# Queries of a gated cross-attention block: where they are split into high and low parts, and how they reach the stacked tile

## The reference

```python
qs = relu(layernorm(x)).reshape(bs, ts, 16, 32);  ks = vs = relu(ctx).reshape(...)
att = softmax(einsum('bthf,byhf->bhty', qs, ks) / sqrt(32))
out = einsum('bhty,byhf->bhtf', att, vs).reshape(bs, ts, -1)
x = x + tanh(g_xattn) * relu(out @ ffn_w.T + ffn_b)
h = layernorm(x);  hp = h shifted by one token
r = sigmoid((mu_r*h + (1-mu_r)*hp) @ W_r.T)
k = square(relu((mu_k*h + (1-mu_k)*hp) @ W_k.T))
x = x + tanh(g_ffn) * r * (k @ W_v.T)
```

## Time and profile before

| | |
|---|---|
| median of three runs | 2981.03 us (2979.23 to 2982.32) |
| the profiled execution | 2980.25 us, its span 2978.4 us |
| PE, matmuls | 2860.3 us busy, 96% of the span |
| PE, weight loads | 2190.6 us, 74% |
| DVE | 2330.1 us, 78% |
| ACT | 1564.3 us, 53% |
| POOL | 1045.4 us, 35% |
| DMA | 408.56 MB, mean 137 GB/s; SP's queue 39.6% of 16 engines, ACT's 7.3% |
| mean granted clock of PE | 0.993 |

### The profile page before, as it was taken

One profiled execution on the slowest core, in us unless ns is written; L12 is line 12 of the kernel. 1 busy time (PEld: TensorE's weight loads), 2 busy tenths in 40 slices (PEclk: granted clock), 3 DMA queues, 4 the chain that ended last, 5 costly groups with the idle time before them and its releaser, 6 DMA issues.

```text
span 2978.4 us, 71298 instructions
## 1 busy us (share of the span) xinstructions
PE 2860.3 (96%) x23168; PEld 2190.6 (74%) x23168; DVE 2330.1 (78%) x4175; ACT 1564.3 (53%) x2828; POOL 1045.4 (35%) x902
## 2 busy tenths in 40 slices
PE   3899999999999999999999999999999999999998
PEld 2677777777777777777777777777777777777776
DVE  5777877878878878878877877877878778788774
ACT  4445555555455455555555555555555555554552
POOL 0233333333343343333333333333333333333434
PEclk9899999999999999999999999999999999999999
DMA  5544445445445445445445445455455454454431
GB/s 168 150 122 140 144 124 155 140 127 155 135 131 156 137 131 154 133 137 150 131 142 149 128 143 153 120 149 152 120 152 146 124 152 142 124 156 137 130 109 41
DMA packets 405258, 408.56 MB, mean 137 GB/s; under 512 B 164577, under 2 KB 329441, under 8 KB 405218
## 3 DMA queue, kind: packets, MB, share of 16 engines
q1 hardware_dynamic: 352994, 340.92, 39.6%
q10 hardware_dynamic: 52224, 67.12, 7.3%
HBM read 272.64 MB, written 134.22 MB: 137 GB/s over the span
## 4 chain that ended last, share of the span: by engine, by line
PE 59%; DVE 16%; DMA 10%; SPq 7%; issue 5%; ACT 1%; ACTq 1%; DVEq 0%; POOL 0%; POOLq 0%
PE bank L951 29%; DMA out_dram<-x 8%; PE bank L918 7%; PE bank L932 6%; PE bank L906 5%; PE bank L944 4%; DVE m_nat L699 4%; DVE o_val L718 4%; SPq L272 3%; DVE st L652 3%; DVE k_raw L682 2%; PE bank L893 2%; PE bank L875 2%; SPq L258 2%; SPq L270 2%
## 5 line engine op out<-in xcount | busy, mean ns | idle before, releaser
L496 ACT ACTIVATE probs<-bank 128x512 f32<-128x512 f32 x1024 | 596.4, 594 | 455.7 <-PE bank L918 228.1
L699 DVE TENSOR_REDUCE m_nat<-bank 128x2 fp32r<-128x512 f32 x1024 | 695.4, 685 | 107.4 <-PE bank L906 106.7
L477 ACT ACTIVATE q_st<-bank 96x512 fp32r<-96x512 f32 x512 | 304.1, 594 | 718.9 <-PE bank L875 718.8
L918 PE MATMUL bank<-q_st,k_st 97*128 97x256 f32 x2048 | 449.9, 301 | 64.2 <-ACT probs L496 47.4
L718 DVE RECIPROCAL o_val<-bank 128x256 f32<-128x256 f32 x256 | 449.1, 1754 | 56.1 <-PE bank L944 51.7
L918 PEld LDWEIGHTS bank<-q_st,k_st 97*128 97x128 f32 x2048 | 341.8, 191 | 153.8 <-issue 58.5
L906 PE MATMUL bank<-k_st,q_st 96*128 96x256 f32 x2048 | 431.6, 293 | 7.4 <-DMA k_st<-k_dram 4.8
L397 POOL TENSOR_TENSOR xm<-xm 128x512 f32<-128x512 f32 x128 | 133.3, 1041 | 787.2 <-ACT xm L540 787.2
L906 PEld LDWEIGHTS bank<-k_st,q_st 96*128 96x128 f32 x2048 | 358.2, 192 | 59.8 <-issue 6.2
L708 DVE CAST m_t<-bank 4x256 fp32r<-4x256 f32 x256 | 105.1, 411 | 285.5 <-PE bank L884 285.4
L364 POOL TENSOR_TENSOR o_lo<-o_mv,o_hi 128x512 fp32r<-128x512 f32 x128 | 164.8, 1287 | 430.0 <-ACT o_hi L503 430.0
(11 more groups left out here) (90 smaller groups left out, 6026.6 us busy)
## 6 DMA issues: line engine op xcount, KB each, us to landing
k_st<-k_dram SPq DMA_DIRECT2D x256, 256.0 KB, 3.6
k_raw<-ctx_t_dram SPq DMA_DIRECT2D x256, 128.0 KB, 3.0
x_ln<-x_dram SPq DMA_DIRECT2D x256, 128.0 KB
k_dram<-k_high SPq DMA_DIRECT2D x64, 512.0 KB, 3.0
k_dram<-k_raw SPq DMA_DIRECT2D x64, 512.0 KB, 4.5
k_st<-k_dram SPq DMA_DIRECT2D x256, 128.0 KB, 3.5
o_dram<-o_val SPq DMA_DIRECT2D x256, 128.0 KB, 1.7
o_mv<-o_dram SPq DMA_DIRECT2D x512, 64.0 KB, 2.2
```

The costliest lines, as they stand in the source:

```text
L477: nc.scalar.activation(q_st[0:QK, c, :, P * u:P * u + P], tp_bank[0:QK, :].rearrange("p (g t) -> p g t", g=GR), ACT.Copy).then_inc(q_stack ...
L496: nc.scalar.activation(probs[:, n // GR % 2, n % GR, :, :].rearrange("p v t -> p (v t)"), st_bank[n % 2][:, :], ACT.Exp, scale=SCALE).then ...
L699: nc.vector.tensor_reduce(m_nat[:, c % 2, :, n % GR:n % GR + 1], s_bank[n % 2][:, :].rearrange("p (u y) -> p u y", u=NU), AX_X, ALU.max, n ...
L918: mm = nc.tensor.matmul(st_bank[n % 2][:, T * v:T * v + T], k_st[0:ST, c, g, P * v:P * v + P], q_st[0:ST, c, g, :], start=True, stop=True)
```

## The change

The queries take the keys' way. `norm_1` writes the normalised values unsplit into `q_nat`, with the features of a group interleaved by head. PE turns each 128x128 block in float32, four blocks to a turn, two turns for a sequence (8 transposes for 32), with no wait for a split. ACT copies each turn out of the bank with a relu (`q_copy`) into `q_raw` and then rounds the whole tile (`q_halve`); DVE subtracts (`q_low`). SP writes both halves to DRAM (`write_q`, behind `write_k`) and reads them back stacked (`stack_q`, behind each `stack_k`). All of it runs one iteration earlier than before, two sequences ahead of the attention.

The core of the diff (declarations, semaphores and the turn table are cut):

```diff
@@ pipeline
-            for i in range(-2, 4):
+            for i in range(-3, 4):
@@ SP
+            def write_q(b, par):
+                if on(b):
+                    sp.wait_ge(q_hi_ready, b + 1)
+                    sp.wait_ge(q_lo_ready, b + 1)
+                    for half, tile in enumerate((q_high, q_raw)):
+                        sp.dma_start(q_dram[par, :, half].rearrange("c f g t -> (f g) c t"),
+                                     tile[:, :, :]).then_inc(q_written, 16)
+            def stack_q(b, c, par):
+                if on(b):
+                    sp.dma_start(q_st[0:HD, c, :, :].bitcast(F32), q_dram[par, c, 0]).then_inc(q_stacked[c], 16)
+                    sp.dma_start(q_st[HD:QK, c, :, :].bitcast(F32),
+                                 q_dram[par, c].rearrange("h f g t -> (h f) g t")).then_inc(q_stacked[c], 16)
             def iteration(i, par):
                 stack_k(i, 3, par)
+                stack_q(i, 3, par)
                 store(i - 3, 1 - par)
                 move_m(i, 1)
...
                 load_k(i + 2)
+                queries_written(i + 1)
                 stack_k(i + 1, 0, 1 - par)
+                stack_q(i + 1, 0, 1 - par)
                 move_m(i, 2)
                 write_o(i, 0)
                 stack_k(i + 1, 1, 1 - par)
-                load_x(i + 2)
+                stack_q(i + 1, 1, 1 - par)
+                load_x(i + 3)
...
                 stack_k(i + 1, 2, 1 - par)
+                stack_q(i + 1, 2, 1 - par)
...
                 write_k(i + 2, par)
+                write_q(i + 2, par)
@@ ACT
-            def q_high(b, u):
...
-            def q_stack(b, c, u):
...
+            def q_copy(b, u):
+                if on(b):
+                    act.wait_ge(q_turned, NU * b + u + 1)
+                    after(act, q_written, 32 * b)
+                    nc.scalar.activation(q_raw[:, :, P * u:P * u + P],
+                                         tp_bank[:, :].rearrange("p (c t) -> p c t", c=CH),
+                                         ACT.Relu).then_inc(q_copied, 1)
+            def q_halve(b):
+                if on(b):
+                    act.wait_ge(q_copied, NU * (b + 1))
+                    nc.scalar.activation(q_high[:, :, :].bitcast(F32R), q_raw[:, :, :], ACT.Copy).then_inc(q_hi_ready, 1)
@@ DVE
+                    after(dve, q_turned, NU * b)
                     for u in range(NU):
-                        nc.vector.tensor_scalar(x_ln[:, u, :], x_ln[:, u, :], mv[:, 0, u, 0:1], rstd[:, 0, u:u + 1],
+                        nc.vector.tensor_scalar(q_nat[:, u, :, :].rearrange("p c (f g) -> p c g f", g=GR),
+                                                x_ln[:, u, :].rearrange("p (c g f) -> p c g f", c=CH, g=GR),
+                                                mv[:, 0, u, 0:1], rstd[:, 0, u:u + 1],
                                                 ALU.subtract, ALU.mult).then_inc(x_normed, 1)
+            def q_low(b):
+                if on(b):
+                    dve.wait_ge(q_hi_ready, b + 1)
+                    nc.vector.tensor_tensor(q_raw[:, :, :].bitcast(F32R), q_raw[:, :, :], q_high[:, :, :],
+                                            ALU.subtract).then_inc(q_lo_ready, 1)
@@ PE
+            def turn_q(b, u, *users):
+                if on(b):
+                    pe.wait_ge(x_normed, NU * b + u + 1)
                     freed(*users)
+                    for c in range(CH):
+                        mm = nc.tensor.transpose(tp_bank[:, P * c:P * c + P], q_nat[:, u, c, :],
+                                                 ident_r[:, :].bitcast(F32))
                     mm.then_inc(q_turned, 1)
@@ scores
-                        pe.wait_ge(q_stacked, 2 * CH * b + 2 * c + 2)
+                        pe.wait_ge(q_stacked[c], 32 * (b + 1))
```

More of the change, by code:

```diff
@@ L56, in flamingo_block @@
         o_dram = nc.dram_tensor("o_dram", [CH, GR, HD, GR, T // GR], F32, kind="Internal").ap()
+        q_dram = nc.dram_tensor("q_dram", [2, CH, 2, HD, GR, T], F32, kind="Internal").ap()
         k_dram = nc.dram_tensor("k_dram", [2, CH, 2, HD, GR, T], F32, kind="Internal").ap()
@@ L139, in flamingo_block @@
         q_turned = sem("q_turned")
-        q_stacked = sem("q_stacked")
+        q_copied = sem("q_copied")
+        q_written = sem("q_written")
+        q_stacked = [sem(f"q_stacked{c}") for c in range(CH)]
         v_ready = sem("v_ready")
@@ L207, in pipeline @@
         def pipeline(eng, iteration):
-            for i in range(-2, 4):
+            for i in range(-3, 4):
                 iteration(i, i % 2)
-            with eng.Fori(6, NB // 2 + 3) as pair:
+            with eng.Fori(6, NB // 2 + 2) as pair:
                 iteration(pair * 2 - 8, 0)
                 iteration(pair * 2 - 7, 1)
-            for i in range(NB - 2, NB + 3):
+            for i in range(NB - 4, NB + 3):
                 iteration(i, i % 2)
@@ L236, in load_x @@
                 if on(b):
-                    after(sp, q_lo_ready, 2 * b)
-                    after(sp, q_hi_ready, 2 * b)
+                    after(sp, x_normed, NU * b)
                     for m in range(GR):
@@ L784, in iteration @@
                 head_max(i, 8)
-                norm_1(i + 1)
+                norm_1(i + 2)
                 split_low(i, 1)
@@ L800, in iteration @@
                 copy_m(i, 2)
-                q_low(i + 1, 1)
                 norm_o(i, 0)
@@ L828, in iteration @@
                 copy_m(i + 1, 0)
+                q_low(i + 2)
                 head_max(i + 1, 4)
-                stats_1(i + 2)
+                stats_1(i + 3)
                 finish(i - 2, 0, par)
@@ L1059, in iteration @@
                 values(i - 1, 3)
-                turn(1)
+                turn(0)
                 denominators(i - 1, 3)
@@ L1064, in iteration @@
                 dense(0, 3)
-                turn(2)
                 shifted_scores(i, 2)
@@ L1072, in iteration @@
                 shifted_scores(i, 3)
-                turn(3)
+                turn(1)
                 dense(1, 2)
@@ L1087, in iteration @@
                 values(i, 0)
-                turn(4)
+                turn(2)
                 denominators(i, 0)
                 shifted_scores(i, 6)
-                turn(5)
                 dense(3, 0)
@@ L1099, in iteration @@
                 scores(i, 14)
-                turn(6)
+                turn(3)
                 dense(3, 3)
@@ L1105, in iteration @@
                 scores(i, 15)
-                turn(7)
                 dense(4, 1)
@@ L1111, in iteration @@
                 values(i, 1)
-                turn(8)
+                turn(4)
                 scores(i + 1, 0)
                 dense(4, 3)
-                turn(9)
+                turn(5)
                 shifted_scores(i, 10)
@@ L1119, in iteration @@
                 denominators(i, 1)
-                turn(10)
+                turn(6)
                 scores(i + 1, 1)
@@ L1127, in iteration @@
                 dense(5, 3)
-                turn(11)
                 shifted_scores(i, 12)
@@ L1137, in iteration @@
                 values(i, 2)
-                turn(12)
+                turn(7)
                 scores(i + 1, 4)
@@ L1145, in iteration @@
                 denominators(i, 2)
-                turn(13)
                 dense(7, 1)
```

69 lines of the change are left out of this document (20 added, 49 removed).

## The result

The changed kernel takes 3407.14 us (median of four runs, 3405.28 to 3409.82); the kernel before, measured beside it, 2980.13. The ratio is 1.143 [1.141, 1.145]: 14% slower, 27 us above the forecast. The profiled execution took 3409.82 us, its span 3407.9.

A forecast was written before the change was run, and what follows sets the result against it. Bound by a loop through the result store in SP's queue. Per iteration 4.51 + 1.14 - 0.78 + 1.68 = 6.55 us, times 60 is 393, plus 8 at the start on 2980.25: forecast 3380 us, range 3250 to 3460.

The forecast's parts named there:

- The loop: Chain from `k_low` through SP's queue, store, ScalarE's exponential and PE back to `k_low`: period from 44.94 to about 51.5 us.
- SP and DMA: SP's queue between `k_low` and store: 1.442 MB of query transfers at 320 GB/s add 4.51 us, bounds 0 and about 5.5.
- The fabric's 435 GB/s: Skill's ceiling for the added bytes: 3.3 us and a total about 70 us lower; the trace's 320 GB/s was preferred.
- Subtract, turns, clock: Per iteration on the loop: DVE's `q_low` adds 1.14 us, fewer PE turns save 0.78, PE's lowered clock adds 1.68.
- PE's wait: PE's wait at `shifted_scores(i, 4)` was to grow from 0.6 to about 6 us.
- ScalarE's wait for the store: Sign to look for: this wait grows by 4 us and more in each of the 60 iterations.
- The start: Queries go to DRAM and back before the first scores, landings of 3.0 and 3.6 plus the subtract: 8 us once.
- The clock did not hold: Rival 1, clock holds: PE's wait grows but PE stays at 2.4 GHz, 3280 us; chance 0.14.
- The store was held back: Rival 2, store not held back: transfers pass each other, only subtract and turns change the loop, 3010 us; chance 0.06.
- PE did not set the end: Rival 3, PE sets the end: loop gets no longer, fewer transposes make it faster, 2895 to 2941 us; chance 0.03.
- The second wait: Rival 4: `move_m(i, 2)` maxima or the output's read come late, up to 1.5 us per iteration more, 3470 us; chance 0.08.

The follow-up runs named there:

- keys_twice: Kernel before, with the two writes of the split keys issued a second time into spare DRAM behind the first: 3306.82 us, ratio 1.110.
- early_write: Changed kernel, with `write_q` moved on SP from behind `write_k` to behind `move_m(i + 1, 0)`: 3127.8 us, ratio 1.050.
- filler: Changed kernel, with 20 unused products of 512 columns on PE ahead of `shifted_scores(i, 4)`: 3321.07 us, ratio 1.115.
- late_reload: Changed kernel, with ScalarE's `load_x1`, which waits for the store, moved from behind `exponent(i, 1)` to behind `exponent(i, 5)`: 3356.92 us, ratio 1.127.
- before_open: Kernel before, with SP's store, `move_m(i, 1)` and `write_o(i - 1, 3)` ahead of `stack_k(i, 3)`, and `load_x1` behind `exponent(i, 5)`: 2885.91 us, ratio 0.968.
- open_loop3: Changed kernel, store and maxima ahead of group 3's stacks, `write_q`, `load_x1`, first query turn moved, `q_low` ahead of `copy_m(i, 3)`, `q_halve` behind `exponent(i, 9)`: 2962.61 us.
- late_stack: Changed kernel, with `stack_q(i, 3)` moved on SP behind the store and `move_m(i, 1)`: 3355.32 us, ratio 1.126.
- dve_slot: Changed kernel, with DVE's `q_low` ahead of `copy_m(i + 1, 0)` instead of behind it: 3372.29 us, ratio 1.132.

## Why the prediction was right, step by step

**The loop.** The period was to grow from 44.94 to about 51.5 by 6.55; it grew by 6.80, from 45.00 to 51.80. The chain runs through the stations foretold, the DMA engines are full for 11.0 us where I had about 10.8, and the queue (keys_twice, early_write) and the clock (filler) were each shown to have their part.

**SP and DMA, 4.51 forecast.** From the keys' write to PE's resumption it is 4.87 more: the store is issued 7.53 us behind that write instead of 3.71, and takes 5.02 to land instead of 4.05. The bytes ahead of it thus delay it twice, at its issue (3.82) and in its landing (0.97); their sum, 4.79, is near the transfer time of 4.51 that I took. It lies inside my bounds of 0 and 5.5, but I had worked out the 5.5 from no row. The fabric's 435 GB/s of the Trainium skill ("DMA: Bandwidth & Descriptors", Specifications) was not reached: the full stretch moved 311, its part from 1040 to 1044 341.

**Subtract, turns, clock: 1.14 - 0.78 + 1.68 = 2.04 forecast, 1.93 measured as their sum.** The filler's trace parts the clock from the other two: PE's resumption to the next keys' write takes 36.03 us there, 37.76 in the changed kernel and 35.85 before (means of 45 settled iterations). So the clock is 1.73 of it, near the 1.68, and the subtract less the turns 0.18 where I had 0.36. The subtract is 1.25 us on the chain, not 1.14; the turns' 0.78 was not measured by itself.

**PE's wait, "about 6".** At `shifted_scores(i, 4)` it is 4.29, with 1.44 and 1.25 just ahead, 6.98 in all. I had written that DVE has done `norm_1` before the wait ends: true, but PE reaches its turn earlier than DVE does, and so stands there first. `norm_1` with its stride takes 743 ns where the plain one took 541 (means of the groups of instructions), and costs nothing in the changed kernel for the reason given.

**ScalarE's wait for the store** grew by (869.9 - 215.4) / 60 = 10.9 us, more than the "4 and more": ScalarE has nothing to do between, and its share of busy time fell to 39%.

**The start: the term that was mis-sized.** I gave it 8 us. PE's timeline, after, at the first scores of all, the first shifted scores and those of head 4 of the first sequence:

```profile
41.99 1.23 PE L921 MATMUL bank<-k_st,q_st 96*128 96x256 f32 x4 [4.44 <-DMA q_st<-q_dram]
...
56.47 0.80 PE L933 MATMUL bank<-q_st,k_st 97*128 97x256 f32 x2 [6.61 <-DMA q_st<-m_t]
...
79.24 0.80 PE L933 MATMUL bank<-q_st,k_st 97*128 97x256 f32 x2 [14.19 <-DMA q_st<-m_t]
```

and of before, the same three places:

```profile
28.72 1.19 PE L906 MATMUL bank<-k_st,q_st 96*128 96x256 f32 x4 [4.76 <-DMA k_st<-k_dram]
...
38.26 0.79 PE L918 MATMUL bank<-q_st,k_st 97*128 97x256 f32 x2 [2.28 <-DMA q_st<-m_t]
...
56.53 0.79 PE L918 MATMUL bank<-q_st,k_st 97*128 97x256 f32 x2 [10.95 <-DMA q_st<-m_t]
```

The delay is 13.3 us at the first scores, 18.2 at the first shifted scores and 22.7 at head 4. By the first store it is 38.1. SP's timeline, after and before:

```profile
64.87 2.34 SPq L281 DMA_DIRECT2D q_dram<-q_high  x1
...
213.37 0.59 SPq L322 DMA_DIRECT2D out_dram<-x  x1
```

```profile
175.24 0.44 SPq L301 DMA_DIRECT2D out_dram<-x  x1
```

So the first scores alone come 13.3 us later, where I had 8; why it is so much more was not traced. The queries' writes then meet the load of the weights (64.87). The iterations ahead of the first store pay for the queue as well, through the maxima, as in late_reload: I had counted only those with a store to wait for. From the first store to the last the difference is (3404.7 - 213.4) - (2975.1 - 175.2) = 391.4 us, where the sum had 393. So the 27 us between forecast and result are the start (30 more) and little else. That 391.4 and 393 lie so close is partly luck: 391.4 is 57.6 periods of 6.80, not 60 of 6.55. The last iterations have no new queries, so the count was too high by as much as the period was too low.

**The rivals.** The clock did not hold (0.50 behind the wait). The store was held back. PE did not set the end; before_open shows what that looks like, and that it needs no change of the queries. The second wait did not open in the changed kernel, but is the one that open_loop3 shows.

## What to carry to other kernels

Before a route is moved onto DMA, look for what stands behind it in the same queue and who waits for that; here a store that somebody waits for turned the transfers ahead of it into time of each iteration. One moved line (early_write) was worth 279 of the 427 us, and a reordering of the kernel before was worth 95, where the transposes saved could give 94 at most. Open the loop first, then ask which engine is next.

## What was not expected of the hardware

- A wait of PE that the profile puts at 0.64 us cost 1.16 by the distances of its products, since those behind it start further apart; and PE that is kept busy with useless products ends 86 us earlier.
- A float32 operation of DVE with two inputs that starts beside GpSimd's subtract takes 2.62 us instead of 0.48, and its neighbours are not slowed. Work taken from DVE to GpSimd gave back 27 of 75 us.
- Moves that take work or bytes off the loop also change how long the clock is low: in late_stack its mean fell by 0.010 and in dve_slot by 0.018, and both gained less than foretold.
- SP's issue of a 512 KB write takes 1.00 to 1.30 us instead of 0.39 to 0.51 where the DMA engines are full: the issuer is held too.
